# A pairwise feature tower: fewer turned units, more summed by ScalarE, GpSimd and VectorE

## The chip, the cores and the metric

The kernel runs on one core of one Trainium2 chip. The metric is the device time of one execution, in microseconds (us); smaller is better. The profile is of one execution.

## The reference

512 samples have 40 categorical features. Each feature's table gives a row of 64 float32 numbers. For every pair of features i < j there is a 64x64 matrix, and the pair's value is the bilinear form of the two rows:

```python
p = inputs[:, rowidx]                       # 780 pairs of 40 features, 64 long
q = inputs[:, colidx]
out = jnp.einsum('bie,fie,bif->bi', p, param, q)
h = jnp.concatenate([z, dense_ctx], axis=1)  # 780 pair values and 16 dense ones
h = jnp.maximum(h @ W_top1 + b_top1, 0.0)    # 796 -> 512
h = jnp.maximum(h @ W_top2 + b_top2, 0.0)    # 512 -> 256
y = h @ W_top3                               # 256 -> 1
```

## The kernel before

**Units.** The batch is cut into two halves (s = 0, 1) of 256 samples. A half's pairs are cut into 100 units, so that there are 200 units, numbered 0 to 199 in the order in which TensorE (PE), and after it VectorE (DVE), take them. A unit holds up to 2048 x 64 products: PE multiplies parameters with gathered rows (into one of three PSUM tiles `upsum`), DVE multiplies the result with the other row of each pair (L660, or L653 and L654 for the small cluster units) and writes it to one of eight slots of `prod`. What is left is a sum over 64 numbers for each pair. Who does it is the unit's letter:

- T and C (turned units, C being the clusters of close pairs): the features lie across the partitions, and PE sums with 8 small matmuls (C: 6) with `sel` into `zbank` (L541), later in the order, one or two units together (`sum_at`).
- S: ScalarE (ACT) sums with 16 pairs of ACTIVATE and accumulator read (L696).
- H: GpSimd (POOL) adds the halves (L445), then DVE reduces what is left (L634, 128x512).
- V: DVE reduces all of it (L634, 128x1024).

PE takes a unit's tile again once the product of three units before is made (from unit 187 = `LAST` on, of two units before; the third tile then holds the last half's layer one). DVE may write unit u's slot only once unit u-8 (`SLOTS`) is summed.

**Who gets which letter.** `cut_units` walks the units with a table `SHARES` (from unit, shares of T, S, V, H), adds the shares to what each letter is owed, and picks by that. The last stretch is all T, and S stops 14 units before the end (`NO_SCALAR`). The letters before, units 0 to 99 and 100 to 199:

```
CTCTSVCSVSVTCSHTSHTTCSHSHTTSHTCSHTTTSHSHTTCSHSHSHTTSHTTTCSHSHSHTTTSHSHTTCSHSHTTSHTTSHSHTTTCSHSHTTTTT
CTCTSHCSHSHTCSHTSHSHCSHSHSHSHTCSHTTTSHSHTTCSHSHSHTTSHTTTCSHSHSHTTTSHSHTTCSHSHTTSHTTSHSHTTTCTTTTTTTTT
```

That is 72 T, 20 C, 54 S, 51 H and 3 V.

**Order on each engine.** Everything is an order written out in advance; each engine goes through the units in turn. ACT comes to unit u's events first and then to the sum of unit u-4 if that is an S (`S_LAG`). DVE reduces a V unit one unit later and an H unit five units later. Between units PE fills a shared bank `abank` (`bank_at`) that ACT empties: turned rows x ("x" one, "xx" two columns of features, L677), "group" (128 pair values of every sample turned for layer one, L679), and the dense layers of the first half ("layer1" x4, "layer2" x2, "layer3" x1). A bank is filled only when its last content is emptied. The full banks of PE's sums (`zbank`) are emptied by ACT as well (L690). The layers of the first half stand at units 113, 122, 126, 133 (layer one), 137, 140 (layer two) and 146 (layer three). From unit 188 on PE takes the second half's layer one, a group at 188, 190, 192, 194, 196 and 198 (`take_group`), and the last one behind the last unit; layers two and three close the kernel.

**Gathers.** POOL issues the 160 indirect DMAs that bring the rows (L428), the first 40 ahead of everything and the others at given units (`gather_at`), in one queue with its H additions. The gathers of features 26 and 27 stand at units 21 and 23; the turn "xx" of columns 12 and 13 (features 24 to 27) stands at unit 30.

Of the kernel before, what the change touches and what calls it, by code (L numbers as in the profile page):

```python
# [35 lines left out]
GATHER_FIRST, GATHER_FROM, GATHER_STEP = 10, 6, 5  # L36
# [5 lines left out]
LAST_UNITS = 13  # L42


SHARES = [(0, 0.55, 0.35, 0.1, 0.0), (14, 0.42, 0.33, 0.0, 0.25)]


def cut_units(N, E, BB):

    owed = {by: 0.0 for by in "TSVH"}
    units, stretches = [], []
    total = 2 * sum((n - n % 2 + 2) // 4 * 2 - (n - n % 2) // 2 % 2 + n % 2 for n in range(N // 2))

    def add(**d):  # L60
        at = [x for x in SHARES if x[0] <= len(units)][-1][1:]
        for by, share in zip("TSVH", at):
            owed[by] += share
        if d["by"] != "C":
            owed[d["by"]] -= 1
        else:
            owed["T"] -= 1
        units.append(dict(d, q=len(stretches) - 1))

    for s in range(2):  # L70
        for n in range(N // 2):
            stretches.append({"s": s, "n": n, "first": len(units), "w": 0 if n % 2 == 0 else 3 * E})
            if n % 2:
                add(s=s, n=n, by="C")
            many = n - n % 2
            for m in range(0, many, 4):
                if many - m < 4:
                    add(s=s, n=n, by="T", m=m)
                    continue
                at = [x for x in SHARES if x[0] <= len(units)][-1][1:]  # L80
                last = n == N // 2 - 1 and (s == 1 or m + 8 > many - 4)
                if last or owed["T"] + at[0] >= 1:
                    add(s=s, n=n, by="T", m=m)
                    add(s=s, n=n, by="T", m=m + 2)
                else:
                    for c in range(2):
                        at = [x for x in SHARES if x[0] <= len(units)][-1][1:]
                        may = [by for by, share in zip("SVH", at[1:]) if share > 0 and (by != "S" or len(units) < total - NO_SCALAR and units[-1]["by"] != "S")]
                        by = max(may, key=lambda by: owed[by])
                        add(s=s, n=n, by=by, m=m, c=2 * s + c)  # L90
            stretches[-1]["end"] = len(units)
    assert len(units) == total


    for s in range(2):
        turned = [d for d in units if d["s"] == s and d["by"] in "TC"]
        groups = -(-len(turned) // (QUAD // 2))
        for x, d in enumerate(turned):
            at = groups * (QUAD // 2) - len(turned) + x
            d["g"], d["r"] = divmod(at, QUAD // 2)  # L100
        flat = {}
        for d in units:
            if d["s"] == s and d["by"] not in "TC":
                d["z"] = flat.setdefault((d["n"], d["m"]), DENSE + 16 * len(flat))
    return units, stretches
# [40 lines left out]
def pairwise_tower_kernel(nc, dense_ctx, ids, tables, param, W_top1, b_top1, W_top2, b_top2, W_top3, out):  # L146
# [12 lines left out]
    units, stretches = cut_units(N, E, BB)  # L159
# [8 lines left out]
    def done_by(kinds, u):  # L168
        return sum(1 for x in units[:u + 1] if x["by"] in kinds)
# [4 lines left out]
    def members(s, g):  # L174
        t = counts[s][0]
        return [u for u in range(NU) if units[u]["s"] == s and
                (units[u]["g"] == g if is_turned(u) else g >= t and units[u]["z"] // P == g - t)]
# [25 lines left out]
    def group_end(s, g):  # L203

        if g < counts[s][0]:
            return max(summed_at[u] for u in members(s, g))
        return max(u + {"S": S_LAG + 5, "V": V_LAG + 3, "H": H_LAG + 2}[units[u]["by"]] for u in members(s, g))
# [18 lines left out]
    for q in range(1, NQ):  # L226
        s, n = stretches[q]["s"], stretches[q]["n"]
        at = stretches[q]["first"]
# [47 lines left out]
    for g in sorted(range(G[1]), key=lambda g: group_end(1, g) if g < counts[1][0] else max(u for u in bank_at if ("group", 1, g) in bank_at[u])):  # L276
        if g != counts[1][0] - 1:
            at = max(after, 2 + (group_end(1, g) if g < counts[1][0] else max(u for u in bank_at if ("group", 1, g) in bank_at[u])))
# [10 lines left out]
    reduce_at = {}  # L289
    for u in range(NU):  # L290
        if units[u]["by"] in "VH":
            reduce_at.setdefault(min(u + (V_LAG if units[u]["by"] == "V" else H_LAG), NU - 1), []).append(u)


    gather_at = {}
    at = GATHER_FROM
    for s, n in [(0, n) for n in range(GATHER_FIRST, NC)] + [(1, n) for n in range(NC)]:
        for x in range(2):
            gather_at.setdefault(at + x * GATHER_STEP // 2, []).append((s, 2 * n + x))
        assert at + GATHER_STEP < [u for u in bank_at if turn_of[(s, n)] in bank_at[u]][0]  # L300
        at += GATHER_STEP

    with ExitStack() as ctx:
# [6 lines left out]
        def sem(name):  # L310
            return ctx.enter_context(nc.semaphore(name))
# [39 lines left out]
        reduced_v = sem("reduced_v")  # L351
        reduced_s = sem("reduced_s")
# [16 lines left out]
        def slot(u):  # L369
            return prod[:, u % SLOTS, :]  # L370
# [77 lines left out]
        def _(pe):  # L448
# [4 lines left out]
            def take_abank():  # L453

                if events[0]:
                    pe.wait_ge(abank_free, events[0])
                events[0] += 1
# [11 lines left out]
            def turn_group(s, g):  # L469
                us = members(s, g)  # L470
                if g == counts[s][0]:
                    pe.wait_ge(dense_in, 16)
                for kinds, done in (("VH", reduced_v), ("S", reduced_s)):
                    mine = [u for u in us if units[u]["by"] in kinds]
                    if mine:
                        pe.wait_ge(done, done_by(kinds, mine[-1]))
                take_abank()
                at = (g - counts[s][0]) * P
                for c in range(PER):
                    last = pe.transpose(abank[0:rows_of(s, g), c * P:(c + 1) * P],  # L480
                                        z[:, s * PER + c, at:at + rows_of(s, g)], ident[:])
                last.then_inc(abank_full, 1)
# [79 lines left out]
            for u in range(NU):  # L562
# [5 lines left out]
                s, n = d["s"], d["n"]  # L568
# [9 lines left out]
                else:  # L578
# [3 lines left out]
                    for x in range(many):  # L582
                        for h in range(2):
# [5 lines left out]
                            else:  # L589
                                at = (d["c"] - s * PER) * P  # L590
# [28 lines left out]
        @block.vector  # L619
        def _(dve):  # L620
            dve.memset(nil[:], 0.0)
            dve.memset(sel[:], 0.0).then_inc(sel_zero, 1)
            dve.wait_ge(sel_zero, 1)
            dve.memset(sel[0:E, QUAD - 2:QUAD - 1], 1.0)
            dve.memset(sel[E:2 * E, QUAD - 1:QUAD], 1.0).then_inc(sel_ready, 1)

            def reduce(u):
                if units[u]["by"] == "H":
                    dve.wait_ge(halved, done_by("H", u))
                    v = slot(u).rearrange("p (q h f) -> p q h f", h=2, f=E // 2)[:, :, 0, :]  # L630
                else:
                    dve.wait_ge(multiplied, u + 1)
                    v = slot(u).rearrange("p (q f) -> p q f", f=E)
                dve.tensor_reduce(z_view(u), v, AX_X, ALU.add).then_inc(reduced_v, 1)  # L634

            for u in range(NU):
                d = units[u]
                s, n = d["s"], d["n"]
                if u >= SLOTS:

                    x = u - SLOTS
                    by = units[x]["by"]
                    if by in "TC":
                        dve.wait_ge(summed, done_by("TC", x))
                    elif by == "S":
                        dve.wait_ge(reduced_s, done_by("S", x))
                    else:
                        dve.wait_ge(reduced_v, done_by("VH", x))
                dve.wait_ge(u_ready, u + 1)
                t = tile(u)  # L650
                to = slot(u)
                if d["by"] == "C":
                    dve.tensor_tensor(to[:, 0:2 * PB], t[:, 0, :], xT[:, s, n - 1:n + 1, :].rearrange("p m b -> p (m b)"), ALU.mult)  # L653
                    dve.tensor_tensor(to[:, 2 * PB:3 * PB], t[:, 1, 0:PB], xT[:, s, n, :], ALU.mult).then_inc(multiplied, 1)  # L654
                else:
                    if d["by"] == "T":
                        f = xT[:, s:s + 1, d["m"]:d["m"] + 2, :].rearrange("p s m b -> p s (m b)")
                    else:
                        f = emb[:, d["c"]:d["c"] + 1, 2 * d["m"]:2 * d["m"] + 8, :].rearrange("p c j f -> p c (j f)")
                    dve.tensor_tensor(to.rearrange("p (h q) -> p h q", h=2), t[:], f.broadcast_to([P, 2, BANK]),  # L660
                                      ALU.mult).then_inc(multiplied, 1)
                for x in reduce_at.get(u, []):
                    reduce(x)
# [115 lines left out]
```

## Time and profile before

| | |
|---|---|
| time, median of 3 | 351.63 us (349.71 to 352.26) |
| the profiled execution | 351.92 us, its span 350.1 us |
| granted TensorE clock, mean | 0.981 |
| instructions | 7011 |

The span runs from the first to the last instruction; 1.8 us of the execution lie around it. A unit's time is found by counting DVE's multiplications (L660, and L653 with L654 as one) in order of time: the first is unit 0, the 186th unit 185. L12 is line 12 of the kernel. "PEld" is PE's weight load.

### The profile page before, as it was taken

What the parts mean: (1) busy time and instruction counts of PE and PEld (TensorE: products, weight loads), DVE (VectorE), ACT (ScalarE), POOL (GpSimd) and SP (SyncE); (2) the same over time, 40 slices, a digit from 0 to 9 for tenths busy, and PEclk for the clock granted to TensorE, in tenths of its full rate; (3) what the DMA queues carried; (4) which work ended last, traced back from release to release, by engine and by line L of the source; (5) the groups of instructions that cost most, each with busy time, mean ns of one, the idle gap of its engine ahead of it and who ended that gap; (6) DMA issues with size and microseconds to landing.
All of it is one profiled execution on the core that took longest, in us unless ns stands there. A gap on an engine that the chain in (4) does not pass through costs nothing.

```text
span 350.1 us, 7011 instructions
## 1 busy us (share of the span) xinstructions
PE 307.4 (88%) x2192; PEld 157.9 (45%) x2192; DVE 261.2 (75%) x278; ACT 230.8 (66%) x1783; POOL 217.2 (62%) x217
## 2 busy tenths in 40 slices
PE   0348838978999999999999999799989999999997
PEld 0123313534444444544654655374544434456665
DVE  0025763994999999999888696947779999986450
ACT  1000854766799489997917798982889988990003
POOL 5777777887788788888867687745676222220000
PEclk9999987998999999999999999989999999999999
DMA  3133595352444443211165343308433234000000
GB/s 77 26 81 89 146 302 160 116 182 53 121 140 136 155 151 94 96 35 36 21 153 149 102 163 106 118 17 323 137 89 115 92 129 147 2 1 3 0 2 0
DMA packets 12935, 35.57 MB, mean 102 GB/s; under 512 B 4705, under 2 KB 5985, under 8 KB 11618
## 3 DMA queue, kind: packets, MB, share of 16 engines
q1 hardware_dynamic: 7778, 29.88, 25.3%
q0 software_dynamic: 5120, 5.25, 7.9%
q8 instruction: 17, 0.28, 0.3%
q14 instruction: 20, 0.16, 0.1%
HBM read 35.12 MB, written 0.00 MB: 100 GB/s over the span
## 4 chain that ended last, share of the span: by engine, by line
PE 56%; issue 12%; DVE 12%; POOL 9%; ACT 8%; DMA 3%; DVEq 0%
PE upsum L591 18%; PE upsum L586 12%; DVE prod L660 10%; PE zbank L541 10%; POOL emb L428 9%; ACT prod L696 7%; PE upsum L485 4%; PE abank L485 3%; PE abank L465 2%; DMA emb<-tbl,rows_id 2%; PE upsum L553 2%; DVE z L634 1%; PE upsum L557 1%; PE abank L521 1%; PE upsum L610 1%
## 5 line engine op out<-in xcount | busy, mean ns | idle before, releaser
L696 ACT ACTIVATE prod<-prod 128x64 f32<-128x64 f32 x864 | 206.4, 243 | 5.9 <-DVE prod L660 5.2
L428 POOL DMA_INDIRECT emb<-tbl,rows_id x160 | 151.6, 948 | 55.1 <-issue 37.2
L696 ACT ACTIVATION_READ_ACCUMULATOR prod<-prod 128x1 f32 x864 | 163.6, 189 | 0.0
L660 DVE TENSOR_TENSOR prod<-upsum,emb 128x1024 f32<-128x1024 f32 x108 | 128.2, 1217 | 26.0 <-PE upsum L591 25.8
L591 PE MATMUL upsum<-w,xT 64*128 64x512 f32 x432 | 115.0, 632 | 3.5 <-DVE prod L660 2.3
L660 DVE TENSOR_TENSOR prod<-upsum,xT 128x1024 f32<-128x1024 f32 x72 | 85.9, 1217 | 27.1 <-PE upsum L586 27.1
L445 POOL TENSOR_TENSOR prod<-prod 128x512 f32<-128x512 f32 x51 | 64.9, 1275 | 39.9 <-DVE prod L660 39.3
L586 PE MATMUL upsum<-xT,w 64*128 64x256 f32 x576 | 79.1, 400 | 2.2 <-DVE prod L660 1.5
L586 PEld LDWEIGHTS upsum<-xT,w 64*128 64x128 f32 x576 | 54.8, 192 | 29.6 <-issue 14.1
L591 PEld LDWEIGHTS upsum<-w,xT 64*128 64x128 f32 x432 | 37.8, 189 | 48.1 <-issue 23.8
L541 PE MATMUL zbank<-prod,sel 128*32 128x256 f32 x696 | 50.8, 386 | 0.0
L465 PE MATMUL abank<-ident,emb 128*128 128x128 f32 x80 | 15.9, 312 | 29.1 <-DMA emb<-tbl,rows_id 25.4
L634 DVE TENSOR_REDUCE z<-prod 128x16 f32<-128x512 f32 (+1 forms) x54 | 38.1, 706 | 0.0
L541 PEld LDWEIGHTS zbank<-prod,sel 128*32 128x32 f32 x696 | 18.2, 109 | 36.5 <-issue 21.0
L653 DVE TENSOR_TENSOR prod<-upsum,xT 128x512 f32<-128x512 f32 x20 | 13.7, 684 | 25.0 <-PE upsum L558 25.0
L675 ACT ACTIVATE xT<-abank 128x256 f32<-128x256 f32 x12 | 4.6, 382 | 41.0 <-PE abank L465 41.0
L465 PEld LDWEIGHTS abank<-ident,emb 128*128 128x128 f32 x80 | 8.8, 150 | 42.8 <-issue 21.6
L485 PE MATMUL abank<-zT,w 128*128 128x256 f32 (+1 forms) x56 | 15.6, 430 | 1.8 <-ACT xT L677 1.8
L690 ACT ACTIVATE zT<-zbank 128x256 f32<-128x256 f32 x6 | 2.3, 376 | 21.8 <-PE zbank L541 21.8
L679 ACT ACTIVATE zT<-abank 128x256 f32<-128x256 f32 (+1 forms) x8 | 3.0, 372 | 20.4 <-PE abank L480 20.4
L677 ACT ACTIVATE xT<-abank 128x512 f32<-128x512 f32 x14 | 8.2, 588 | 12.2 <-PE abank L465 12.2
L553 PE MATMUL upsum<-xT,w 64*64 64x256 f32 x40 | 13.6, 423 | 2.2 <-ACT xT L675 1.9
(42 smaller groups left out, 168.3 us busy)
## 6 DMA issues: line engine op xcount, KB each, us to landing
w<-W_top SPq DMA_DIRECT2D x2, 1792.0 KB, 9.1
emb<-tbl,rows_id POOLq DMA_INDIRECT x160, 2.5
w<-param SPq DMA_DIRECT2D x2, 1248.0 KB
w<-param SPq DMA_DIRECT2D x2, 1152.0 KB
w<-param SPq DMA_DIRECT2D x2, 1120.0 KB
w<-param SPq DMA_DIRECT2D x2, 1024.0 KB
w<-param SPq DMA_DIRECT2D x2, 992.0 KB
w<-param SPq DMA_DIRECT2D x2, 896.0 KB
```

The lines of the kernel that those rows point to most:

```text
L428: pool.indirect_dma_start(emb[:, c, f, :], None, tables[f], bass.IndirectOffsetOnAxis(ap=rows_id[:, c, f:f + 1].bitcast(U32), axis=0),).th ...
L445: pool.tensor_tensor(p[:, :, 0, :], p[:, :, 0, :], p[:, :, 1, :], ALU.add).then_inc(halved, 1)
L465: last = pe.transpose(abank[:, x * PB + c * P:x * PB + (c + 1) * P], emb[:, s * PER + c, 2 * (n + x):2 * (n + x) + 2, :].rearrange("p i e ...
L485: return pe.matmul(to, w1[0:rows_of(s, g), g, m * P:(m + 1) * P], zT[0:rows_of(s, g), room(s, g), :], start=start, stop=stop)
L541: last = pe.matmul(zbank[t * QUAD:(t + 1) * QUAD, 0:PB], sel[:, QUAD - 2 - 2 * d["r"]:2 * QUAD - 2 - 2 * d["r"]], slot(u)[:, t * PB:(t + 1 ...
L553: pe.matmul(t[0:E, 0, 0:PB], ws[hi, 0:E], xT[hi, s, n - 1, :], start=True, stop=True)
L586: last = pe.matmul(tile(u)[:, h, x * PB:(x + 1) * PB], w[rows, x_load % W_SLOTS, base + x * P:base + (x + 1) * P], xT[rows, s, n, :], star ...
L591: last = pe.matmul(tile(u)[:, h, :], xT[rows, s, n, at:at + P], w[rows, x_load % W_SLOTS, base:base + BANK], start=True, stop=True)
L634: dve.tensor_reduce(z_view(u), v, AX_X, ALU.add).then_inc(reduced_v, 1)
L653: dve.tensor_tensor(to[:, 0:2 * PB], t[:, 0, :], xT[:, s, n - 1:n + 1, :].rearrange("p m b -> p (m b)"), ALU.mult)
L660: dve.tensor_tensor(to.rearrange("p (h q) -> p h q", h=2), t[:], f.broadcast_to([P, 2, BANK]), ALU.mult).then_inc(multiplied, 1)
L696: last = act.activation(ring[:, x * E:(x + 1) * E], ring[:, x * E:(x + 1) * E], ACT.Copy, accum_out=z_view(u)[:, x:x + 1])
```

## The change

Two edits. The table of shares has four entries in place of two. The rule of `cut_units` then gives these letters:

```
CTCTSVCSVSVTCSHTSHSHCSHSVTTSHTCSHSHTSVTTSHCSHSHTTSHTTSHTCSVSHSHTTTSHSHTTCSVSHSHTTSHTTSHSVTCSHSHTTTTT
CTCTSHCSHSHTCSHTSHSHCSHSHSHSVTCSHSHTSHSHSHCSHSVSHSHSHSHTCSHSHSHTSHSHSHSHCSHSHSHSHSHTTSHHHTCTTTTTTTTT
```

That is 50 T, 20 C, 64 S, 56 H and 10 V. Units 0 to 17 and 100 to 127 keep their letters. The first half has 40 turned units (46 before), the second 30 (46), so that the second half fills two banks of PE's sums and five groups in place of three and four; there are seven inputs of layer one for each half as before. Of the events, the first half's groups move from units 61 and 99 to 55 and 83, the second half's stand at 149, 152, 169, 187 and 196 (149, 155, 183 and 195 before), and the sums' banks are emptied at 18, 66, 102, 158 and 202 (32, 68, 102, 138, 180 and 202). Layers, turned rows, gathers and `take_group` stay at their units.

The second edit counts DVE's reductions in the order in which DVE makes them (`vector_order`), since a V unit now overtakes an H unit; the waits of PE and DVE use that count. The rounding of `gather_at` gives the same units as before.

```diff
-SHARES = [(0, 0.55, 0.35, 0.1, 0.0), (14, 0.42, 0.33, 0.0, 0.25)]
+SHARES = [(0, 0.45, 0.4, 0.15, 0.0), (12, 0.37, 0.38, 0.03, 0.22), (100, 0.22, 0.4, 0.05, 0.33), (150, 0.28, 0.37, 0.0, 0.35)]
...
+    vector_order = [u for at in sorted(reduce_at) for u in reduce_at[at]]
+    vector_count = {u: x + 1 for x, u in enumerate(vector_order)}
...
-            gather_at.setdefault(at + x * GATHER_STEP // 2, []).append((s, 2 * n + x))
+            gather_at.setdefault(int(at + x * GATHER_STEP / 2), []).append((s, 2 * n + x))
...
-                for kinds, done in (("VH", reduced_v), ("S", reduced_s)):
-                    mine = [u for u in us if units[u]["by"] in kinds]
-                    if mine:
-                        pe.wait_ge(done, done_by(kinds, mine[-1]))
+                mine = [u for u in us if units[u]["by"] in "VH"]
+                if mine:
+                    pe.wait_ge(reduced_v, max(vector_count[u] for u in mine))
+                mine = [u for u in us if units[u]["by"] == "S"]
+                if mine:
+                    pe.wait_ge(reduced_s, done_by("S", mine[-1]))
...
-                        dve.wait_ge(reduced_v, done_by("VH", x))
+                        dve.wait_ge(reduced_v, vector_count[x])
```

## Rows read from the trace of the kernel before

**Rows 1.** The page's first part: busy us, share of the span, instructions.

```profile
PE 307.4 (88%) x2192; PEld 157.9 (45%) x2192; DVE 261.2 (75%) x278; ACT 230.8 (66%) x1783; POOL 217.2 (62%) x217
```

**Rows 2.** The page's chain that ended last, share of the span by engine.

```profile
PE 56%; issue 12%; DVE 12%; POOL 9%; ACT 8%; DMA 3%; DVEq 0%
```

**Rows 3.** Busy time by stretch: us, each engine (instructions), granted clock, DMA.

```profile
139.00:163.00 24.00, 23.02 (x179) 11.44 (x181) 24.00 (x27) 24.00 (x199) 20.25 (x20) 1.00 0.25 75
163.00:177.00 14.00, 14.00 (x128) 7.90 (x120) 12.95 (x15) 9.52 (x68) 11.46 (x12) 1.00 0.17 36
177.00:211.00 34.00, 33.94 (x253) 17.77 (x251) 26.72 (x32) 22.00 (x166) 24.27 (x24) 1.00 0.49 138
211.00:227.00 16.00, 14.82 (x81) 7.33 (x77) 13.30 (x15) 15.90 (x129) 12.23 (x12) 1.00 0.40 122
227.00:233.00 6.00, 5.25 (x19) 4.08 (x21) 2.09 (x3) 4.56 (x36) 4.56 (x5) 0.72 0.09 18
233.00:247.00 14.00, 14.00 (x100) 7.82 (x99) 9.57 (x9) 5.91 (x40) 6.32 (x6) 1.00 0.56 211
247.00:262.00 15.00, 13.82 (x99) 6.38 (x96) 12.49 (x13) 13.89 (x112) 10.15 (x11) 1.00 0.37 110
262.00:309.00 47.00, 45.56 (x342) 20.89 (x340) 46.28 (x50) 43.59 (x354) 16.62 (x15) 1.00 0.27 96
309.00:350.00 41.00, 38.27 (x292) 25.38 (x288) 19.07 (x19) 10.32 (x65) 2.40 (x2) 1.00 0.00 1
```

**Rows 4.** Groups by line and shape: busy us, mean ns, idle before.

```profile
L696 ACT ACTIVATE prod<-prod 128x64 f32<-128x64 f32 x864 | 206.4, 243 | 5.9 <-DVE prod L660 5.2 <-issue 0.7
...
L445 POOL TENSOR_TENSOR prod<-prod 128x512 f32<-128x512 f32 x51 | 64.9, 1275 | 39.9 <-DVE prod L660 39.3
...
L541 PE MATMUL zbank<-prod,sel 128*32 128x256 f32 x696 | 50.8, 386 | 0.0
...
L677 ACT ACTIVATE xT<-abank 128x512 f32<-128x512 f32 x14 | 8.2, 588 | 12.2 <-PE abank L465 12.2
...
L679 ACT ACTIVATE zT<-abank 128x256 f32<-128x256 f32 x6 | 2.2, 371 | 4.3 <-PE abank L480 4.3
```

**Rows 5.** The chain in order of time: start us, us, what, count.

```profile
193.47 3.20 PE abank L485 x13
...
227.75 4.95 PE abank L485 x13
...
240.54 1.00 PE zbank L541 x16
...
244.23 1.94 PE abank L521 x8
...
246.67 7.64 ACT prod L696 x64
```

**Rows 6.** The same chain about unit 185's multiplication.

```profile
308.70 1.23 DVE prod L660
...
309.97 1.14 PE upsum L586 x8
```

**Rows 7.** GpSimd in order of time: unit 22, and the last gather of feature 27.

```profile
72.85 1.29 POOL L445 TENSOR_TENSOR prod<-prod 128x512 f32<-128x512 f32 x1
...
75.56 0.94 POOL L428 DMA_INDIRECT emb<-tbl,rows_id  x1 [0.31 <-issue]
```

**Rows 8.** TensorE in order of time, the turn ahead of unit 30.

```profile
80.25 0.63 PE L465 MATMUL abank<-ident,emb 128*128 128x128 f32 x4 [3.75 <-issue]
```

**Rows 9.** VectorE in order of time, a V and an H reduction and what follows.

```profile
42.90 1.21 DVE L634 TENSOR_REDUCE z<-prod 128x16 f32<-128x1024 f32 x1
44.03 1.22 DVE L660 TENSOR_TENSOR prod<-upsum,emb 128x1024 f32<-128x1024 f32 x1
...
304.71 0.68 DVE L634 TENSOR_REDUCE z<-prod 128x16 f32<-128x512 f32 x1
305.31 1.22 DVE L660 TENSOR_TENSOR prod<-upsum,xT 128x1024 f32<-128x1024 f32 x1
```

## Prediction

> **What bounds the kernel now.** I read the engines' shares first: TensorE is busy 88% of the span, VectorE 75%, ScalarE 66%, GpSimd 62% [rows 1], and the chain that ended last is TensorE for 56% [rows 2]. Read alone, these say that TensorE is the bound, and that taking sums from it pays. So the next view has to be the stretches, because the engines take turns [rows 3]. From 139 to 163 us VectorE has no idle time (24.00 of 24.00). From 163 to 211 TensorE has none, or nearly none (14.00 of 14.00, 33.94 of 34.00). From 211 to 227 ScalarE works 15.90 of 16.00. From 233 to 247 it is nearly idle, 5.91 of 14.00, since it waits for TensorE's layer two. From 262 to 309 VectorE works 46.28 of 47, but ScalarE 43.59 as well: the two are close to equal there, and that is what the whole change turns on. From 309 on TensorE works 38.27 of 41.
>
> **What one unit costs each engine.** ScalarE sums two S units in 7.64 us [rows 5], 3.82 each; the ACTIVATE group says the same (206.4 us for 54 units, 3.82) [rows 4]. The sum on TensorE that an S unit saves is 50.8 us for 92 turned units, 0.55 each [rows 4]. GpSimd's addition for an H unit is 1.28 us [rows 4]. Behind an H reduction VectorE's next instruction starts 0.60 us after it (305.31 minus 304.71), behind a V reduction 1.13 us (44.03 minus 42.90) [rows 9]. The multiplications and the large matmuls are the same for every letter, so they drop out.
>
> **Totals.** 22 fewer T units take 22 x 0.55 = 12 us from TensorE. 10 more S units put 10 x 3.82 = 38 us on ScalarE; 5 more H units put 6.4 us on GpSimd and 3.0 on VectorE, 7 more V units 7.9 on VectorE. What counts is where these lie.
>
> **Start, units 0 to 29.** Units 0 to 17 are unchanged. The stretch ends where TensorE, after 3.75 us of idling, turns the rows of features 24 to 27 at 80.25 [rows 8]. Its last gather was issued at 75.56, behind unit 22's addition [rows 7], in one queue on GpSimd that is full. Unit 19 is now an H, and its addition stands in that queue ahead of the gathers of features 26 and 27: 1.3 us later. The two T units that leave here only lengthen TensorE's idling. So +1.3 us, between 0 (if the landing, not the issue, was late) and +3 (if the longer idling costs clock, see below).
>
> **Units 30 to 99.** Up to 163 us VectorE sets the pace or nearly does. It gets: a V at 37 (+1.13), a V for an H at 58 (+0.53), V at 74 and 88 with one H fewer (+1.66). Together +3.3 us; the bound below is +1, if its small gaps early in the stretch take the first two. GpSimd has fewer additions from 57 on, not more. ScalarE has ten S units more in all, but three here, and the group that kept unit 57's sum waiting at 61 has moved to 55, which starts that sum earlier; counted through by 3.82 each, no slot of the eight comes free late before unit 100. From 163 to 177 TensorE is the bound, and two sums that stood at 91 are gone: 1.0 us off. Sum: +1.3 + 3.3 - 1.0 = +3.6 us at unit 100. Units 100 to 127, layer one and ScalarE's chain at 211 are unchanged, so this is carried on unaltered. What is bounded is 0 to +6.
>
> **Units 128 to 140.** The chain runs over TensorE here, up to the second matmul group of layer two at 244.23, and ScalarE's sum of unit 136 starts behind it at 246.67 [rows 5]. Three turned units' sums leave the stretch (1.00 at 240.54 and the 0.57 of a single unit), so that 136 starts 1.6 us earlier, at 245.1. The new S unit 133 (3.82 us) fits into ScalarE's idle stretch, 233 to 247 [rows 3], and costs nothing; the rest of that idle time stays unused, since layer two's events stand before the sums in ScalarE's order.
>
> **Units 136 to 185: the decisive sum.** From here ScalarE has these S units up to 177: 136, 138, 140, 143, 145, 147, 149, 151, 153, 157, 159, 161, 164, 166, 168, 170, 173, 175, 177. That is 19 x 3.82 = 72.6 us. Among them it empties three banks of 512 columns (0.59 each) and five of 256 (0.37 each, layer three and the emptied sums taken as the group's) [rows 4]: 3.6 us. 245.1 + 72.6 + 3.6 = 321.3 us. VectorE can write unit 185's product only when unit 177's slot is free, and in the kernel before that product starts at 308.70 [rows 6]. So it now ends at 321.3 + 1.23 = 322.5, not at 309.93: +12.6 us. VectorE alone would not be late: with its added reductions it would have some 4 us more here, which lie beside ScalarE's work. Nor can the ring absorb it. Between 247 and 309 ScalarE idled 1.1 + 3.4 us [rows 3], while the sums from 136 to 177 are six more than before (19 for 13), 22.9 us; what of that the ring and the idle time take up is already in the difference of 12.6.
>
> **The end.** TensorE's matmul of unit 187 starts right behind that product, at 309.97 [rows 6], and from there on TensorE is the bound for 40.2 us (38.27 busy of 41) [rows 3]. That stretch has as many sums and groups as before: one pair of sums moves from 191 to 187, group five's turn now stands at 187 but lies in the wait. The H units 187 and 188 add reductions behind TensorE's pace. So the end moves by the same 12.6 us.
>
> **The edit of the counts** costs nothing: VectorE waits for a count of its own earlier instructions, and TensorE's groups wait for members several units old. The letters' order is what the counts must follow, not a new wait.
>
> **Sum.** 350.1 + 3.6 + 12.6 = 366.3 us of span, with 1.8 us around it 368.1, which is 16.2 us above the profiled 351.92. The median shown, 351.63, lies 0.3 below that execution, so I predict 351.63 + 16.2 = 367.8 us.
>
> **TensorE's clock.** Its granted mean was 0.72 in 227 to 233 us, behind a wait for ScalarE [rows 3], and thirteen matmuls of layer one took 4.95 us there against 3.20 at full clock [rows 5]: one such fall costs 1.75 us if TensorE is then the bound. With ScalarE the bound TensorE would be busy for about 52 of 75 us (59.4 minus 14 x 0.55), in short bursts, and the end follows on directly. Within ScalarE's stretch a fall is hidden; at its end it costs 1.75 us. The Trainium skill ("TensorE: Matmul & The Clock Gate", section "HAM oscillation") warns of just this, bursts of matmuls parted by waits that bring the clock down again and again; the row at 227 us agrees for a single wait. I leave it out of the forecast, because where the fall lands is open.
>
> **Rivals.**
> *ScalarE's surplus is absorbed.* If the eight slots and the idle time before 262 took all of the added sums, only VectorE's added reductions would show: +3.6 in the first half and from unit 146 on one V in place of an H and five H (0.53 + 3.0): 351.6 + 3.6 + 3.5 = 358.7 us. For it: ScalarE had 8.1 us idle in 233 to 247. Against: it is idle because of layer two's events, and ahead of it ScalarE worked 15.90 of 16.00 us, so it enters the gap late with its sums, not early [rows 3]. Chance 0.13.
> *The clock falls at the start of the end, and perhaps at unit 30.* 367.8 + 1.75 = 369.6, with both 371.3. Chance 0.22.
> *TensorE was the bound all the way.* If the 12 us of sums came off the path, the time would be 351.6 - 12 = 339.6 us. The mechanism is TensorE's queue between the large matmuls; it decides if ScalarE gets its 38 us into time in which it idled. ScalarE's idle 119 us in all [rows 1] speak for it. Against: from 139 us on only two stretches hold much of it, 233 to 247 (8 us, behind layer two's events) and 309 to 350 (31 us, where S units are not allowed), and of the TensorE-bound stretches only 163 to 177 loses turned units' sums [rows 3]. Chance 0.05.
> *The change doesn't act as counted* (ScalarE's sums faster or slower in the denser order, GpSimd late for the reductions): 0.05, with no time of its own.
> The forecast has 0.55. The range goes from 357, which takes in most of the first rival, to 372, which takes in the second and the upper bound of the first half.
>
> **Chances.** No change is anything within 1%, about what a measurement of this kernel can tell. Faster 0.05, same 0.04, slower 0.91.
>
> **What would show it.** After: ScalarE with next to no idle time from the sum of unit 136 to that of 185; S units waiting longer and longer behind their products; VectorE idle before the products of units whose number less eight is an S, from about 153 to 185; unit 185's product about 16 us later (325), unit 100's about 3.6 later. TensorE's sums x520 in place of x696, and its end stretch still 40 us. The prediction is wrong if ScalarE shows gaps there, or if unit 100 comes earlier than before.

## The result, and the profile after

The changed kernel took 362.16 us (median of 4, 358.66 to 365.63) against 351.94 us before: ratio 1.027, interval 1.018 to 1.036. In a later comparison over more executions it was 361.72 against 350.57, ratio 1.042 (1.034 to 1.049). The kernel before lay between 346.41 and 353.24 us there, so its profiled execution, 351.92, is one of its longer ones; what that does to the sizes is told below. The profiled execution is 361.88 us with a span of 359.9, 9.8 us longer than the span before. Ratios leave disturbed runs out, so they are not always the quotients of the medians.

The engines' shares, which answer to [rows 1]:

```profile
PE 303.5 (84%) x1930; PEld 144.9 (40%) x1930; DVE 271.7 (76%) x290; ACT 267.7 (74%) x2103; POOL 223.7 (62%) x222
```

TensorE lost only 3.9 us of busy time, not 12, though its sums are x520 in place of x696, as counted. At least a part of this is the clock: in this execution it was at half for 28.5 us, in the one before for 14.7. ScalarE gained 37, as counted. The shares are as silent on the bound as those before. The stretches, with the columns of [rows 3], are not:

```profile
177.00:209.00 32.00, 31.94 (x224) 16.92 (x222) 25.15 (x29) 22.18 (x167) 23.43 (x23) 1.00 0.47 136
209.00:225.00 16.00, 14.75 (x80) 7.19 (x78) 13.37 (x15) 16.00 (x131) 10.45 (x10) 1.00 0.40 123
225.00:240.00 15.00, 14.53 (x76) 8.71 (x76) 11.15 (x12) 12.71 (x99) 10.05 (x10) 1.00 0.48 174
240.00:262.00 22.00, 19.47 (x100) 6.93 (x100) 20.23 (x22) 21.74 (x175) 16.35 (x17) 1.00 0.38 126
262.00:316.00 54.00, 40.61 (x196) 14.41 (x192) 44.45 (x48) 54.00 (x445) 20.57 (x17) 0.91 0.20 71
316.00:324.00 8.00, 7.08 (x30) 3.46 (x30) 4.76 (x5) 8.00 (x68) 2.53 (x2) 0.57 0.00 0
324.00:359.00 35.00, 33.23 (x253) 22.51 (x252) 15.81 (x16) 7.47 (x41) 1.27 (x1) 1.00 0.00 1
```

From 262 to 316 us ScalarE has not a moment idle (54.00 of 54.00), while VectorE, the busiest there before, is down to 44.45 of 54 and TensorE to 40.61 with its clock at 0.91. Just after, 316 to 324, the clock is 0.57. The chain in order of time (start, us, what) says the same in one look:

```profile
238.30 1.94 PE abank L526 x8
240.24 0.02 issue
240.26 0.47 ACT h L688
240.74 7.63 ACT prod L701 x64
248.37 0.48 ACT xT L682
248.85 3.82 ACT prod L701 x32
252.67 0.26 ACT yT L690
252.92 3.82 ACT prod L701 x32
256.74 0.27 ACT zT L684
257.01 7.64 ACT prod L701 x64
264.65 0.26 ACT zT L684
264.91 11.45 ACT prod L701 x96
276.36 0.48 ACT xT L682
276.84 0.26 ACT zT L695
277.10 15.28 ACT prod L701 x128
292.38 0.26 ACT zT L684
292.64 11.46 ACT prod L701 x96
304.10 0.48 ACT xT L682
304.58 11.47 ACT prod L701 x96
316.05 0.03 issue
316.07 1.23 DVE prod L665
317.31 0.04 issue
317.35 2.08 PE upsum L596 x4
319.43 1.86 PE zbank L546 x16
321.29 2.90 PE upsum L490 x8
```

Counted in 32 instructions a unit (16 ACTIVATE, 16 accumulator reads) these are the 19 sums of units 136 to 177, 3.82 us each, with the emptied banks between them and nothing else. At 316.05 the slot of unit 177 is free and VectorE's product of unit 185 starts at 316.07. In [rows 5] and [rows 6] that path went over VectorE and ended at 308.70.

Unit by unit, VectorE's products against those before: unit 29 is 3.0 us later, unit 30 1.1 earlier, unit 57 1.2 earlier, unit 100 1.5 earlier, unit 133 4.0 earlier, unit 140 5.9 earlier, unit 164 2.3 later, unit 185 7.4 later, unit 199 9.8 later. So the first 140 units gained, and the next 45 lost 13 us.

What happened ahead of unit 30 was not foreseen. Before, TensorE idled 3.75 us until 80.25 [rows 8]. After, GpSimd in order of time:

```profile
75.37 0.95 POOL L431 DMA_INDIRECT emb<-tbl,rows_id  x1 [0.16 <-issue]
76.63 0.94 POOL L431 DMA_INDIRECT emb<-tbl,rows_id  x1 [0.30 <-issue]
```

and TensorE's turn, with no idle time before it:

```profile
79.47 0.66 PE L468 MATMUL abank<-ident,emb 128*128 128x128 f32 x4
```

The last gather of feature 27 was 1.07 us later than the 75.56 of [rows 7], as predicted up to 0.2, and yet the turn was 0.8 us earlier. The DMA view of 76 to 80 us shows why. Of the kernel before:

```profile
q1 hardware_dynamic: 144, 0.88, 66.5%
q0 software_dynamic: 90, 0.09, 9.4%
```

and of the changed one (packets, MB, share of the 16 DMA engines; q1 is SyncE's loads, q0 the gathers):

```profile
q0 software_dynamic: 78, 0.09, 14.7%
q1 hardware_dynamic: 7, 0.05, 9.2%
```

Before, the 0.88 MB of parameters of column 13 moved just then, beside the gather that TensorE waited for. After, that load was issued at 78.6 in place of 75.5 us, since the matmuls of unit 29, which free its buffer, came later. The gather was issued by 77.57, a microsecond ahead of it.

### The profile page after: what moved, and what is told of

It is laid out like the page before. It is cut to its first block, busy times and chain, and to the rows that moved or that the text cites. A ratio compares the mean times of both kernels' runs of the same rounds, so it can differ in the third digit from the quotient of the medians.

```text
span 359.9 us, 6824 instructions
## 1 busy us (share of the span) xinstructions
PE 303.5 (84%) x1930; PEld 144.9 (40%) x1930; DVE 271.7 (76%) x290; ACT 267.7 (74%) x2103; POOL 223.7 (62%) x222
## 4 chain that ended last, share of the span: by engine, by line
PE 35%; ACT 26%; DVE 13%; POOL 12%; issue 10%; DMA 3%; DVEq 0%
ACT prod L701 24%; POOL emb L431 11%; PE upsum L596 10%; DVE prod L665 10%; PE upsum L591 7%; PE zbank L546 6%; PE upsum L490 4%; DVE z L639 3%; PE abank L490 3%; DMA emb<-tbl,rows_id 2%; PE abank L468 1%; PE upsum L558 1%; PE abank L526 1%; POOL prod L448 1%; PE upsum L615 1%
## 5 line engine op out<-in xcount | busy, mean ns | idle before, releaser
L701 ACT ACTIVATE prod<-prod 128x64 f32<-128x64 f32 x1024 | 244.6, 243 | 0.9 <-DVE prod L665 0.9
L701 ACT ACTIVATION_READ_ACCUMULATOR prod<-prod 128x1 f32 x1024 | 194.3, 190 | 0.0
L665 DVE TENSOR_TENSOR prod<-upsum,emb 128x1024 f32<-128x1024 f32 x130 | 154.2, 1215 | 38.4 <-PE upsum L596 32.4
L596 PE MATMUL upsum<-w,xT 64*128 64x512 f32 x520 | 139.1, 638 | 12.1 <-DVE prod L665 10.6
L665 DVE TENSOR_TENSOR prod<-upsum,xT 128x1024 f32<-128x1024 f32 x50 | 59.8, 1214 | 16.3 <-PE upsum L591 15.0
L591 PE MATMUL upsum<-xT,w 64*128 64x256 f32 x400 | 57.5, 413 | 4.3 <-DVE prod L665 3.6
L591 PEld LDWEIGHTS upsum<-xT,w 64*128 64x128 f32 x400 | 38.5, 197 | 28.7 <-DVE prod L665 14.0
L639 DVE TENSOR_REDUCE z<-prod 128x16 f32<-128x512 f32 (+1 forms) x66 | 49.7, 755 | 0.0
L558 PE MATMUL upsum<-xT,w 64*64 64x256 f32 x40 | 13.7, 423 | 3.4 <-ACT xT L680 1.9
L490 PE MATMUL upsum<-zT,w 128*128 128x256 f32 (+1 forms) x56 | 14.8, 411 | 0.5 <-ACT zT L695 0.5
L559 PE MATMUL upsum<-xT,w 64*64 64x256 f32 x40 | 13.8, 427 | 0.0
```

What stands on the lines that cost most here:

```text
L490: return pe.matmul(to, w1[0:rows_of(s, g), g, m * P:(m + 1) * P], zT[0:rows_of(s, g), room(s, g), :], start=start, stop=stop)
L558: pe.matmul(t[0:E, 0, 0:PB], ws[hi, 0:E], xT[hi, s, n - 1, :], start=True, stop=True)
L559: pe.matmul(t[E:2 * E, 0, 0:PB], ws[lo, 0:E], xT[lo, s, n, :], start=True, stop=True)
L591: last = pe.matmul(tile(u)[:, h, x * PB:(x + 1) * PB], w[rows, x_load % W_SLOTS, base + x * P:base + (x + 1) * P], xT[rows, s, n, :], star ...
L596: last = pe.matmul(tile(u)[:, h, :], xT[rows, s, n, at:at + P], w[rows, x_load % W_SLOTS, base:base + BANK], start=True, stop=True)
L701: last = act.activation(ring[:, x * E:(x + 1) * E], ring[:, x * E:(x + 1) * E], ACT.Copy, accum_out=z_view(u)[:, x:x + 1])
```

## The experiments

Letters were set by a written-out string in place of `SHARES`; all else is the changed kernel's code. The edits are shown in short. Ratios are against the kernel before on the same chip.

**The first half alone.**

```diff
-SHARES = ...
+LETTERS = new[0:100] + old[100:200]
```

> The new letters for units 0 to 99, the old ones for 100 to 199. Theory A (the first half gains because the stall ahead of unit 30 is gone, and the whole loss is ScalarE's in the second half): unit 100's product about 2 us earlier than before and the end with it, 349.8 us, ratio 0.994. Theory B (the forecast's sum for the first half, +3.6 us, holds on average and the one execution was lucky): 355 us.

348.10 us, ratio 1.001 (0.996 to 1.006). In its profile unit 100's product comes at 175.3 us (176.9 before, 175.5 in the changed kernel), unit 185's at 304.6, span 346.0. That is theory A's place for unit 100 in the execution profiled, and theory B's loss of 3.6 us is not there. Over all executions it is no faster than the kernel before, which, run 23 times there, spread from 346.49 to 352.90. What the stall cost in each of those isn't recorded, since only one execution of it is profiled. So a gain of the first half is shown against that one execution only, not against the kernel before as a whole.

**The second half alone.**

```diff
+LETTERS = old[0:100] + new[100:200]
```

> The old letters for units 0 to 99, the new ones for 100 to 199. Theory A: unit 100 as before; from there the loss of the changed kernel without its 2 us of gain: unit 185's product some 9 to 10 us late, 361 to 365 us with the clock's falls. Theory B (the loss is shared by both halves): 358 us or less.

361.82 us, ratio 1.029 (1.022 to 1.035), unit 100 at 177.6 and unit 185 at 319.0 us. The whole loss is in the second half; theory B for the halves falls. The stall ahead of unit 30 is there again: TensorE idled 3.58 us before the turn, which came at 80.92 us.

**Shorter sums on ScalarE.**

```diff
-                for x in range(16):
+                for x in range(12 if 133 <= u <= 185 else 16):
```

> The changed kernel, but each S unit from 133 to 185 sums only 12 of its 16 columns on ScalarE (the others are left at zero, so part of the computation is left out). That takes 4 x 0.239 = 0.96 us from each of 19 sums between units 136 and 177. Theory A (ScalarE's capacity sets unit 185): the 18 us come off ScalarE's chain until VectorE or TensorE is the bound again; unit 185's product at about 306 to 308 us, and the whole 349 to 352 us. Rival (VectorE's added reductions and the order of the banks set it): within 2 us of the changed kernel, 360 us.

347.66 us, ratio 0.996 (0.991 to 1.001); unit 185's product at 303.7 us, 12.4 earlier than in the changed kernel. Nothing but ScalarE's time per unit was taken (the columns that it leaves are set to zero at the start, so the kernel leaves out part of the sums), with the same letters, banks and reductions. Its stretches:

```profile
262.00:303.00 41.00, 36.24 (x180) 12.29 (x178) 41.00 (x46) 41.00 (x336) 18.84 (x16) 1.00 0.26 91
303.00:344.00 41.00, 37.72 (x284) 24.88 (x282) 21.17 (x22) 7.42 (x38) 3.76 (x3) 1.00 0.00 1
```

VectorE is at 41.00 of 41 again. With all of its added reductions it reaches unit 185 no later than before (303.7 us). So ScalarE's capacity is shown to be the cause.

**Some pairs given back.**

```diff
+LETTERS = new, but T T at 153, 154 and 164, 165      (two pairs)
+LETTERS = new, but T T also at 149, 150 and 170, 171 (four pairs)
```

> The changed kernel with two of its S and H pairs in the second half (units 153 and 154, 164 and 165) made T again, as before. Theory A (ScalarE's capacity between 136 and 177): 2 x 3.82 = 7.6 us off unit 185's product (308.5 in place of 316.1) and off the end, 353 to 355 us. Rival (the order as a whole, reductions and banks, costs it): two of seven pairs give back two sevenths of the loss, some 3 us, 359 us.

357.70 us, ratio 1.028 (1.017 to 1.039). Unit 185's product at 310.0 us in an execution whose clock was at half from 225.5 to 228.9, where unit 133 already came 1.5 us later than in the changed kernel: from unit 133 to 185 it took 78.5 us against 86.1, that is 7.6 less for two pairs. The slope of 3.82 for each S unit is right. The profiled execution is some 3 us above what I had expected: 1.5 us stand there at unit 185, and behind it the clock was at half once more (3.4 us from 310.8) and the rest to unit 199's product took 32 us, where it took 30.4 before. That the falls are what the 3 us are is likely by their size, not shown.

> As the last, with four pairs made T again (149, 153, 164 and 170 with their neighbours). Theory A: ScalarE would come 15 us earlier, more than it is late, so VectorE and TensorE are the bound again: unit 185's product at 304 to 306 us, 348 to 351 us, as with the old letters in the whole second half. Rival: four sevenths, 356 us.

348.68 us, ratio 1.001 (0.996 to 1.006), unit 185 at 303.9 us. ScalarE and VectorE are level then:

```profile
262.00:304.00 42.00, 39.42 (x266) 17.05 (x262) 41.28 (x45) 41.30 (x336) 15.45 (x13) 1.00 0.25 90
```

The loss is gone with three of the seven added S units still there. So the point from which ScalarE decides lies between three and five added units between 133 and 185.

**TensorE given more to do.**

```diff
+                    again = 2 if d["by"] in "HV" and 141 <= u <= 186 else 1
...
-                    for x in range(many):
+                    for x in [x for x in range(many) for _ in range(again)]:
```

> The changed kernel, with the large matmuls of the H and V units from 141 to 186 issued twice (same result written again): 0.96 us more for TensorE for each, 23 units, some 22 us of work, in the time in which TensorE waits. Theory A (ScalarE is the bound there and TensorE's waits bring its clock down, which costs at the end): no later product of unit 185, no half clock after 270 us, the end stretch from 187's product 40.2 in place of 42.5 us; 358 to 360 us. Rival (TensorE's work counts there): 365 us or more.

362.00 us (358.55 to 363.69), ratio 1.040 (1.031 to 1.049). Unit 185's product at 315.6 us against 316.1: the added matmuls moved nothing, so TensorE is not the bound there. (They are 80 matmuls of 20 units, not of 23 as counted above: by the price of 0.96 us for each unit some 19 us. TensorE's busy time grew by 9.9 us only, from 303.5 to 313.4, with less of it at half clock.) The clock:

```profile
262.00:315.00 53.00, 48.35 (x258) 20.89 (x254) 45.26 (x49) 53.00 (x436) 20.75 (x18) 0.97 0.20 72
315.00:356.00 41.00, 37.61 (x284) 24.85 (x282) 20.56 (x21) 16.06 (x112) 3.80 (x3) 1.00 0.00 1
```

In this execution it was 0.97 in ScalarE's stretch and full at the end, and from unit 187's product to the end 37.2 us passed in place of 40.0. (The 40.2 and 42.5 us of the expectation are measured from unit 187's matmuls, not from its product.) That looked like theory A, so both went once more, side by side:

> The changed kernel itself, beside the next one on the same chip, for a median over more executions: 360 to 363 us, ratio 1.03.

361.72 us (360.33 to 364.25), ratio 1.042.

> The changed kernel with the doubled matmuls once more, beside the changed kernel. If keeping TensorE busier holds its clock, 2 to 3 us below the changed kernel's median here; if its clock falls as often in either, the same within 1 us. More than 2 us above it would mean that TensorE's added work is on the path after all.

362.34 us (358.61 to 364.43), ratio 1.040. No difference in the median. That more work for TensorE saves the clock is not shown. That a fall at the end costs some 2.5 us there is: both profiles of the changed kernel have the clock at half for 6.8 us around 316 us and need 40.0 and 39.7 us from unit 187's product on, both with doubled matmuls have it full and need 37.2.

**The load and the gather.** The letters before in both halves, with one wait:

```diff
+                if (d["s"], d["n"]) == (0, 13):
+                    sp.wait_ge(gathered[0][13], 16 * 2 * PER)
                 sp.dma_start(w[:, x % W_SLOTS, 0:cols], ...
```

> The kernel before, with one wait more: SyncE issues the parameter load of column 13 only when the gathers of features 26 and 27 have landed. Theory A (the stall of 3.75 us ahead of unit 30 was that load's packets in front of the gather's): the turn at 78.0 to 78.5 in place of 80.25 us, perhaps no fall of the clock at 81 us, 348 to 350 us. Rival (the gather was late by itself or TensorE waited for something else): the turn at 80.2 and 351.9 us.

346.75 us, ratio 0.990 (0.984 to 0.995): faster than the kernel before by 1%, the only one of these kernels whose interval lies below 1. TensorE's turn in order of time, and the stretch that follows:

```profile
78.00 0.63 PE L459 MATMUL abank<-ident,emb 128*128 128x128 f32 x4 [1.43 <-issue]
```

```profile
82.00:86.00 4.00, 4.00 (x38) 2.81 (x36) 3.50 (x5) 4.00 (x33) 3.51 (x4) 1.00 0.15 32
```

1.43 us of idling in place of the 3.75 of [rows 8], and the clock stays at 1.00. In the kernel before the same 4 us read:

```profile
82.00:86.00 4.00, 4.00 (x19) 1.40 (x17) 2.64 (x4) 3.32 (x28) 3.52 (x4) 0.65 0.14 24
```

Unit 57's product is 3.8 us earlier (114.7 for 118.5). Its executions lie between 346.39 and 348.05, those of the kernel before beside it between 346.49 and 352.90: the wait takes the long executions away and leaves the shortest as they were. Theory A is shown. The run with old letters in the first half and no such wait ("The second half alone") stalled like the kernel before, so the rest of the changed kernel's code is not what helped; and as the shortest executions are the same, the edit of the counts costs nothing, as forecast.

> The new letters for the first half, the old ones for the second, and the parameter load of column 13 held until the gathers of features 26 and 27 have landed. If the new letters' gain in the first half was only that the load came later by itself, holding adds nothing to them and this stands with the kernel before with the load held, 346.5 to 348 us, ratio 0.99. If the letters gain something of their own, 344 to 345 us.

347.60 us (347.51 to 349.26), ratio 0.999 (0.995 to 1.003); unit 100's product at 175.0 us against 173.2 with the old letters and the same wait. With the stall out of the way the new letters cost the first half 1.8 us; they gained nothing of their own. On the way the products of these two runs lie 1.1 us apart at unit 30, 3.2 at unit 90, 1.8 at unit 100 and 1.2 from unit 110 to 126.

**Together.** Old letters in the first half, four pairs given back in the second, the load held.

> The version that the runs point to: the old letters in the first half, the load of column 13 held, and in the second half the new letters with four pairs made T again (three more S units than before). From unit 100 to 185 the runs gave 128.8 us with these letters and 130.1 with the old ones: 345.5 to 346.5 us, about 1 us under the kernel before with the load held, 0.985 to 0.99 of the kernel before. Rival: ScalarE's order gives that microsecond back at the end, 346.5 to 347.5.

347.32 us (345.70 to 349.00), ratio 0.997 (0.993 to 1.001). The profiled span is the shortest of all, 343.9 us, and from unit 100 to 185 it took 129.5 us for 130.1. That is not enough to tell it from the old letters with the load held, and it does not clearly beat the kernel before. The median lies in the rival's range, but its mechanism isn't seen in the profile: from unit 185 to 199 it took 30.2 us, against 30.4 with the old letters. That three more S units are a gain or a loss is not shown.

## Why the prediction held, and where it was off

Forecast 367.8 us, 16.2 above the time before; measured 9.8 above it in the profiled spans, 10.2 in the medians. The direction, the main mechanism and the place were right; the terms beside the main one were not. They were too long by 5.7 us (first half, read at unit 126) and 2.3 us (units 128 to 140) and too short by 2.4 us (the end), so that they cancel in part, and the measured time lies in the range but nearer to the first rival's 358.7 than to the forecast. What decides between the two is ScalarE's chain, not the time. Most of what lies between 16.2 and 9.8 is the kernel before's own loss in its profiled execution: the letters before with the load held had a span of 344.7 us, 5.4 less than the 350.1 that the forecast starts from and 15.2 less than the changed kernel's. Of the forecast's own signs, ScalarE without a gap, the sums x520 and a late unit 185 came; one of its two signs of being wrong came as well: unit 100 was 1.5 us earlier than before, not 3.6 later.

*Units 136 to 185, the decisive sum.* 76.2 us were counted for ScalarE's chain, 75.3 passed (240.74 to 316.05). A bank that ScalarE empties took 0.26 or 0.48 us of the chain, not 0.37 and 0.59. That this chain is the cause is shown from two sides: shorter sums with everything else kept (12.4 us earlier), and the slope of 7.6 us for two pairs. That VectorE's added reductions lie beside it is shown by the same run.

*The first half.* This step failed: +3.6 was forecast, 2.1 us of gain came (unit 126). The forecast's start term had the gather later by 1.3 us, and it was, by 1.07, but it took the wait's end in the kernel before for the gather's natural landing. That wait was lengthened by a collision with column 13's load, which cost the kernel before 3.8 us at unit 100 (173.2 us with the load held); the forecast's own lower bound of 0 did not reach to a gain. The row with 3.75 us of idling stood there, and TensorE started 3.7 us after the end of the gather's issue at 76.5, which should have raised the question of what else moved then. Once the collision is taken out of both, the letters cost +1.8 at unit 100, half of the +3.6: the start term came to +1.1 (forecast 1.3), VectorE's from unit 30 to 90 to +2.1 (3.3), and behind the sums that are gone 1.3 came off by unit 100 (1.0) and 0.6 more by unit 110, where none was forecast. Why the last came off is open.

*Units 128 to 140.* 1.6 us earlier was forecast relative to unit 126, 3.9 came (unit 136's sum from 246.67 to 240.74, of which 2.1 are the first half's). The letters' part is 2.0: from unit 136's product to unit 140's it took 7.1 us in place of 9.1, and 9.1 in the run with the first half alone. The other 1.9 lie between the products of units 126 and 133 and are mostly layer one's matmuls at unit 133:

```profile
225.47 3.29 PE abank L490 x14
```

where [rows 5] has 4.95, since the clock did not fall there in this execution. It did in the run with two pairs given back, so this part is chance. The first half's and this term together explain 8 us of difference.

*The end.* 0 forecast, +2.4 came: the chain's last rows above show the four matmuls of unit 187 in 2.08 us, where four such took 1.06 us at full clock at 228.77; then sixteen small ones of sums in 1.86 (1.00 in [rows 5]) and eight of layer one in 2.90. Before, eight of layer one took

```profile
311.10 1.92 PE upsum L485 x8
```

These three are 2.9 us longer together, with the clock at half for 6.8 us from 316.4. That is the second rival's mechanism at its place, together with the forecast's main one; the forecast had left it out, with 1.75 us as its price.

In the changed kernel's stretch 262 to 316 the clock was 0.91, where it was 1.00 from 262 to 309 in [rows 3], and TensorE stood still for 13.4 of the 54 us. The Trainium skill ("TensorE: Matmul & The Clock Gate", section "HAM oscillation — how this bites in real kernels") has bursts parted by waits bring the clock down again. The trace agrees so far as the clock fell where TensorE waited more; but the fall at 272.0 came ahead of the longest wait (3.62 us, from 273.6 to 277.2), and the longest in the ten microseconds before it was 1.30 us. Whether more work for TensorE would hold it up stays open; the two runs with doubled matmuls gave no lower median.

*Rivals.* Absorption by the eight slots (358.7 us) is refuted by ScalarE's 54.00 of 54 and by the shorter sums. TensorE as the bound all the way (339.6) is refuted by the direction, and for the decisive stretch by the doubled matmuls: unit 185 came at 315.6 and 316.1 us in their two profiles, against 316.1 and 315.9.

## What to carry to other kernels

When two engines are near balance in a stretch, count the candidate engine's work in that stretch alone, from the event that starts it to the slot that frees the next consumer: 19 x 3.82 us plus the banks gave the path to 1 us, while the shares of the whole span (66% for ScalarE) said there was room. Take more than one execution of the kernel before: its profile held a stall that its shortest executions, by their times, seem not to have had. A wait for a DMA in the kernel before is not a constant: look at what else the queues moved in those microseconds before carrying it on, since moving one compute step moves the load that it frees. And a stall may cost twice, once by itself and once by the clock that falls behind it: 2.3 us less of waiting brought unit 57 on by 3.8.

## What the runs showed of the hardware

- With 0.88 MB of a parameter load beside it (144 packets of q1 from 76 to 80 us), TensorE got a gather's rows 3.7 us after the end of its issue; with the load held behind it, TensorE's turn came at 78.00 us, 2.25 us earlier. In the two profiles with the old letters and the load held the turn came at 78.00 and 78.03 us, in the two without at 80.25 and 80.92. The wait on SyncE was worth 1% of the kernel (ratio 0.990).
- The kernel before ran at 346.4 to 353.1 us over 23 executions on one chip, its mean granted clock 0.985 to 0.990 in those under 347 us and 0.976 in those over 352: for how long the clock was at half differs from one execution to the next. With the load held the spread was 1.7 us (6 executions) and 1.8 us (12, with the new letters in the first half), but 3.3 us in the last kernel above, so the stall is not all of it.
- TensorE's clock was at half for 10.2 us from 272.0 in the changed kernel; in the ten microseconds before, TensorE was busy for 7.47, and the longest wait was 1.30 us. The 3.62 us wait came when the clock was already down. This fall cost nothing, since ScalarE was the bound; the one at 316.4 did.
